# Relative scores of the first cross stream in nine full runs of 512 columns instead of twelve chunks, staged in four slots

## The reference, cut to what matters

```python
q = (einsum('bsd,ed->bse', query, Wq) + bq).reshape(B, S, H, dh).transpose(0, 2, 1, 3)   # H = 16, dh = 32; k and v alike
QEr  = einsum('bhsd,ld->bhsl', q, Er)          # relative scores: row s against all 1024 distances
Srel = _skew(QEr)                              # shifts row s so that distances become key positions
attn = (einsum('bhsd,bhtd->bhst', q, k) + Srel) / sqrt(dh)
attn = softmax(where(causal, attn, -inf))      # causal: key t <= query s
out  = einsum('bhst,bhtd->bhsd', attn, v)
```

## Time and profile before

| | us |
|---|---|
| median of 3 runs | 4168.61 (4167.6 to 4168.93) |
| span of the profiled execution, first to last instruction | 4166.1 |
| PE busy in it | 3837.0 (92%) |
| DVE busy | 2484.1 (60%) |
| ACT busy | 1563.3 (38%) |
| POOL busy | 908.5 (22%) |
| mean granted TensorE clock, as a share of full speed | 0.977 |

### The profile page before, as it was taken

The page is one execution under the profiler, slowest core; times in us unless marked ns, Lnnn a source line. Parts: engine busy times, 40 slices in busy tenths (PEclk is TensorE's granted clock), DMA queues, the critical chain, the costliest instruction groups (busy, mean ns, idle before and its releaser), DMA issues. The chain is left out here.

```text
span 4166.1 us, 90771 instructions
## 1 busy us (share of the span) xinstructions
PE 3837.0 (92%) x36668; PEld 2320.9 (56%) x36668; DVE 2484.1 (60%) x4832; ACT 1563.3 (38%) x3158; POOL 908.5 (22%) x1023
## 2 busy tenths in 40 slices
PE   5999998989999989999999899999998948999995
PEld 2667644656775456567754565677545623444442
DVE  3777535877774358777744587777445872222224
ACT  2444224854442257544422575444135730000002
POOL 2333100223331002233310022333100202222221
PEclk8999999999999999999999999999999978999998
DMA  8333349744333497443335963433359624666667
GB/s 257 109 94 96 119 177 337 234 132 112 96 96 109 189 337 229 131 115 95 95 102 198 344 224 119 115 95 95 102 216 339 221 88 125 157 147 156 149 154 232
DMA packets 325767, 680.63 MB, mean 163 GB/s; under 512 B 28753, under 2 KB 128129, under 8 KB 322129
## 3 DMA queue, kind: packets, MB, share of 16 engines
q1 hardware_dynamic: 272848, 620.60, 46.2%
q0 software_dynamic: 15344, 35.46, 4.6%
q10 hardware_dynamic: 37184, 19.02, 2.1%
HBM read 389.36 MB, written 210.11 MB: 144 GB/s over the span
## 5 line engine op out<-in xcount | busy, mean ns | idle before, releaser
L523 ACT ACTIVATE sc<-sc,nmax 128x1024 f32<-128x1024 f32 x516 | 591.7, 1147 | 774.7 <-DVE nmax L749 774.2
L480 POOL TENSOR_SCALAR sc<-sc,pinv 128x1024 f32<-128x1024 f32 x516 | 576.5, 1118 | 1196.2 <-DVE pinv L757 1183.0
L1081 PE MATMUL psum<-pts,wct 32*64 32x256 f32 x8192 | 460.2, 376 | 9.2 <-PEq L1076 5.2
L1081 PE MATMUL psum<-xall,wct 32*64 32x256 f32 x8192 | 458.7, 376 | 6.9 <-issue 6.8
L1066 PE MATMUL psum<-xt,w_all 128*128 128x256 f32 x1792 | 415.7, 385 | 23.5 <-PEq L1063 23.5
L879 DVE CUSTOM_DVE_ANT_0 sc<-psum,big 128x896 f32<-128x896 f32 (+7 forms) x512 | 364.0, 753 | 104.7 <-PE psum L1287 89.5
L774 DVE STREAM_TRANSPOSE pts<-sc 128x1024 f32<-128x1024 f32 (+3 forms) x342 | 333.6, 976 | 128.2 <-PE psum L1081 84.8
L1066 PEld LDWEIGHTS psum<-xt,w_all 128*128 128x128 f32 x1792 | 332.5, 190 | 128.2 <-issue 66.9
L523 ACT ACTIVATE sc<-sc,xmax 128x896 f32<-128x896 f32 (+7 forms) x512 | 394.8, 773 | 11.7 <-DVE xmax L879 11.6
L749 DVE CUSTOM_DVE_ANT_0 sc<-psum,table_a 128x1024 f32<-128x1024 f32 x258 | 312.1, 1210 | 111.7 <-PE psum L1024 95.9
L1081 PEld LDWEIGHTS psum<-pts,wct 32*64 32x64 f32 x8192 | 310.4, 132 | 100.1 <-issue 55.2
(11 more groups left out here) (175 smaller groups left out, 5242.4 us busy)
## 6 DMA issues: line engine op xcount, KB each, us to landing
wct<-xall SPq DMA_DIRECT2D x576, 128.0 KB, 2.4
big<-skew_d SPq DMA_DIRECT2D x48, 1024.0 KB, 5.9
w_sb<-w_dram SPq DMA_DIRECT2D x48, 1024.0 KB, 5.5
big<-skew_d SPq DMA_DIRECT2D x48, 768.0 KB, 4.4
big<-skew_d SPq DMA_DIRECT2D x32, 896.0 KB, 4.6
big<-skew_d SPq DMA_DIRECT2D x32, 640.0 KB, 5.4
w_all<-wqkv_dram SPq DMA_DIRECT2D x33, 512.0 KB, 3.6
skew_d<-pts SPq DMA_DIRECT2D x8, 2048.0 KB, 6.6
```

What stands on the lines that cost most here:

```text
L480: pool.tensor_scalar(sc[k % 4][:, :], sc[k % 4][:, :], pinv[:, k % 4:k % 4 + 1], 1.0, ALU.mult, ALU.mult).then_inc(probs_scaled, 1)
L523: act.activation(tile, tile, ACT.Exp, bias=least, scale=-1.0, accum_out=total).then_inc(probs_ready, 1)
L1081: mm = pe.matmul(OSUM[HEAD[h], a, :], v_all[rows, ST * (b % GROUPS) + b // GROUPS, HEAD[h]], ptf[h][rows, QG * b:QG * b + QG], start=(b == ...
```

## The change

The 12 chunks of a quad become 9 runs (RUNS), each with exactly 512 columns of PSUM. Six runs are a whole piece of one tile as before. Three runs join pieces of two tiles: 384 columns of tile 6 with the first 128 of tile 4, 256 of tile 5 with the 256 of tile 1, 384 of tile 2 with the 128 of tile 0. The products are the same 12 pieces a quad. Ahead of every run TensorE makes two eighths (FILL = 2): 36 runs, the same 72 eighths. ACT and DVE copy a joined run in two instructions and signal once, behind the second.

The stores are bound to runs (REL_STORES): tile 7 behind run 1, tile 6 behind run 3, tiles 5 and 1 behind run 5, tile 4 behind run 6, tile 3 behind run 7, tiles 2 and 0 behind run 8 (the last). The staging has four slots (REL_SLOT), each used twice a quad: `pts` for tiles 7 and 4, `wct` for 6 and 3, columns 0 to 767 of `big[4:8]` for 5 and 2, and columns 768 to 1023 of it for 1 and 0. The two waits ahead of the second stream change with them: ACT and DVE wait for slots 0 and 1 in full, SP for slots 2 and 3 in full before the load of unit 2. The loads of units 0 and 1 stay behind the last store of the second quad. The diff, without what only renames counts (copy_rel of ACT has the same edit as that of DVE):

```diff
-REL_ORDER = [7, 6, 5, 4, 3, 2, 1, 0]
-CHUNKS = [(t, n) for t in REL_ORDER for n in range(0, P * (t + 1), HALF)]
-NCH = len(CHUNKS)
-FILL = [2 if min(HALF, P * (t + 1) - n) == HALF else 1 for t, n in CHUNKS] * QUADS
-FILLED = [sum(FILL[:kk]) for kk in range(len(FILL) + 1)]
+RUNS = [[(7, 0, 512)], [(7, 512, 512)], [(6, 0, 512)], [(6, 512, 384), (4, 512, 128)], [(5, 0, 512)],
+        [(5, 512, 256), (1, 0, 256)], [(4, 0, 512)], [(3, 0, 512)], [(2, 0, 384), (0, 0, 128)]]
+NRUN = len(RUNS)
+REL_STORES = [(1, (7,)), (3, (6,)), (5, (5, 1)), (6, (4,)), (7, (3,)), (8, (2, 0))]
+REL_SLOT = {7: (0, 0), 4: (0, 1), 6: (1, 0), 3: (1, 1), 5: (2, 0), 2: (2, 1), 1: (3, 0), 0: (3, 1)}
+FILL = 2
+SPLIT = 6 * P
...
-        rel_stored = [sem(f"rel_stored{i}") for i in range(3)]
+        rel_stored = [sem(f"rel_stored{i}") for i in range(4)]
...
-            return next((r for r in range(3, len(BLOCKS)) if FILLED[kk] < ST * (r - 2) <= FILLED[kk + 1]), None)
+            done = FILL * (kk + 1)
+            return 2 + done // ST if done % ST == 0 else None
+
+        def rel_slot(t):
+
+            return relb[min(REL_SLOT[t][0], 2)][:, :, 0 if t > 1 else SPLIT:S]
+
+        def rel_uses(qd, t):
+
+            return 2 * qd + REL_SLOT[t][1]
+
+        def pieces(j):
+
+            return [(t, n, m, sum(p[2] for p in RUNS[j][:i])) for i, (t, n, m) in enumerate(RUNS[j])]
...
-                    made = qd * ST + REL_ORDER.index(t)
-                    sp.wait_ge(rel_stored[made % 3], 16 * (made // 3 + 1))
+                    sp.wait_ge(rel_stored[REL_SLOT[t][0]], 16 * (rel_uses(qd, t) + 1))
...
-                for v in range(XV):
-                    t = REL_ORDER[v % ST]
-                    w = width(t)
-                    made = NCH * (v // ST) + max(j for j in range(NCH) if CHUNKS[j][0] == t) + 1
-                    sp.wait_ge(rel_by_act, made)
-                    sp.wait_ge(rel_by_dve, made)
-                    sp.dma_start(skew_d[v - v % ST + t, 0:HPQ * P * w].rearrange("(h p n) -> p h n", h=HPQ, p=P),
-                                 relb[v % 3][:, :, 0:w]).then_inc(rel_stored[v % 3], 16)
-                    if v == 2 * ST - 1:
+                for qd in range(QUADS):
+                    for j, tiles in REL_STORES:
+                        sp.wait_ge(rel_by_act, NRUN * qd + j + 1)
+                        sp.wait_ge(rel_by_dve, NRUN * qd + j + 1)
+                        for t in tiles:
+                            w = width(t)
+                            sp.dma_start(skew_d[qd * ST + t, 0:HPQ * P * w].rearrange("(h p n) -> p h n", h=HPQ, p=P),
+                                         rel_slot(t)[:, :, 0:w]).then_inc(rel_stored[REL_SLOT[t][0]], 16)
+                    if qd == 1:
                         load_skewed(0)
                         load_skewed(1)
-                sp.wait_ge(rel_stored[2], 16 * len(range(2, XV, 3)))
+                sp.wait_ge(rel_stored[2], 16 * 2 * QUADS)
+                sp.wait_ge(rel_stored[3], 16 * 2 * QUADS)
...
-                        sp.wait_ge(rel_stored[1], 16 * len(range(1, XV, 3)))
+                        sp.wait_ge(rel_stored[1], 16 * 2 * QUADS)
...
-                act.wait_ge(rel_stored[0], 16 * len(range(0, XV, 3)))
+                for i in range(2):
+                    act.wait_ge(rel_stored[i], 16 * 2 * QUADS)
...
-                    t, n = CHUNKS[j]
-                    v, m = qd * ST + REL_ORDER.index(t), min(HALF, width(t) - n)
-                    dve.wait_ge(rel_for_dve, NCH * qd + j + 1)
-                    if v >= 3:
-                        dve.wait_ge(rel_stored[v % 3], 16 * (v // 3))
-                    dve.tensor_copy(relb[v % 3][:, 2:4, n:n + m], psum[:, 6:8, 0:m]).then_inc(rel_by_dve, 1)
+                    dve.wait_ge(rel_for_dve, NRUN * qd + j + 1)
+                    for t, n, m, at in pieces(j):
+                        if rel_uses(qd, t) > 0:
+                            dve.wait_ge(rel_stored[REL_SLOT[t][0]], 16 * rel_uses(qd, t))
+                        ins = dve.tensor_copy(rel_slot(t)[:, 2:4, n:n + m], psum[:, 6:8, at:at + m])
+                    ins.then_inc(rel_by_dve, 1)
 
                 copy_block(1)
...
-                dve.wait_ge(rel_stored[0], 16 * len(range(0, XV, 3)))
+                for i in range(2):
+                    dve.wait_ge(rel_stored[i], 16 * 2 * QUADS)
...
-                    t, n = CHUNKS[j]
-                    w, k = width(t), NCH * qd + j
-                    m = min(HALF, w - n)
+                    k = NRUN * qd + j
                     if j == 0:
                         pe.wait_ge(*evacuated(BLOCKS.index((0, qd))))
                     pe.wait_ge(rel_by_act, k)
                     pe.wait_ge(rel_by_dve, k)
-                    for h in range(HPQ):
-                        mm = pe.matmul(psum[:, 4 + h, 0:m], xq[DH * h:DH * h + DH, qd, P * t:P * t + P],
-                                       er_sb[DH * h:DH * h + DH, S - w + n:S - w + n + m], start=True, stop=True)
-                        if h == 1:
-                            mm.then_inc(rel_for_act, 1)
+                    for t, n, m, at in pieces(j):
+                        first, last = S - width(t) + n, at + m == HALF
+                        for h in range(HPQ):
+                            mm = pe.matmul(psum[:, 4 + h, at:at + m], xq[DH * h:DH * h + DH, qd, P * t:P * t + P],
+                                           er_sb[DH * h:DH * h + DH, first:first + m], start=True, stop=True)
+                            if last and h == 1:
+                                mm.then_inc(rel_for_act, 1)
                     mm.then_inc(rel_for_dve, 1)
...
                 for qd in range(QUADS):
-                    for j in range(NCH):
-                        kk = NCH * qd + j
-                        for i in range(FILLED[kk], FILLED[kk + 1]):
+                    for j in range(NRUN):
+                        for i in range(FILL * (NRUN * qd + j), FILL * (NRUN * qd + j + 1)):
                             project_eighth(3 + i // ST, i % ST)
                         relative(qd, j)
```

More of the change, by code:

```diff
@@ L455, in _ @@
                 sp.sem_inc(x2_ready, -1)
-                for i in range(3):
-                    sp.sem_inc(rel_stored[i], -16 * len(range(i, XV, 3)))
+                for i in range(4):
+                    sp.sem_inc(rel_stored[i], -16 * 2 * QUADS)
                 def store_rows(dst):
@@ L634, in copy_rel @@
                 def copy_rel(qd, j):
[L636 to L641 removed]
+                    act.wait_ge(rel_for_act, NRUN * qd + j + 1)
+                    for t, n, m, at in pieces(j):
+                        if rel_uses(qd, t) > 0:
+                            act.wait_ge(rel_stored[REL_SLOT[t][0]], 16 * rel_uses(qd, t))
+                        ins = act.copy(rel_slot(t)[:, 0:2, n:n + m], psum[:, 4:6, at:at + m])
+                    ins.then_inc(rel_by_act, 1)
                 root_of_variance()
@@ L1361, in _ @@
                 pe.sem_inc(ot_scaled, -XV)
[L1362 to L1363 removed]
+                pe.sem_inc(rel_by_act, -NRUN * QUADS)
+                pe.sem_inc(rel_by_dve, -NRUN * QUADS)
                 for c in range(DC):
```

23 lines of the change are left out of this document (8 added, 15 removed).

## The result

The changed kernel takes 4183.64 us (median of 5 runs, 4181.85 to 4186.94); the kernel before, on the same chip, 4168.93 (5 runs, 4167.6 to 4172.29). The ratio is 1.0036, with a 95% interval of 1.0023 to 1.0048. The forecast was 4153, its range 4133 to 4176.

The account below looks back on a forecast made before the run. PE, busy 92% of the span, was taken as the bound, with DMA 81% busy in the stage. 12.6 won - 6.0 store waits - 2.4 border = 4.2 us a batch, 16 in all: 4153 us, range 4133 to 4176.

Parts of the forecast that it names:

- PE's side: Relative-product stage: fewer alternations, joined groups costing 0.1 us each; 107.6 us without other holds, 12.6 us a batch won.
- Tile 7's store before run 4: In the stage, tile 4's first copy waits for this store to free the slot; 0.7 us lost in every quad.
- waits of copies other than tile 4's: Sign in the changed kernel's profile that would show the forecast wrong; no size given.
- The queue: Stores between quads: queue runs to 31.7 us, next tile 7 starts at 33.1; waits including tile 7's, 6.0 us a batch.
- an odd late store: In the stage's store queue: delays about once a quad, 0 to 1.8 us each, taken as 1.2, sometimes two.
- The clock: Rival: the third quad's wait lowers PE's clock, costing 5 us a batch there and about 2 at the border; chance 0.10.
- The border: Start of the second stream: first addition loses 0.8 us and unit 2 1.6; together 2.4 us a batch, bounds 0 and 5.
- the first addition: Start of the second stream: waits for tiles 4 and 3, 5.6 us behind the last product, a loss of 0.8.
- unit 2's load: Second stream: waits for tiles 2 and 0, issued at 8.5 us, takes 3.4; unit 2's addition 12.7, loss 1.6.
- later units have more room: Second stream behind unit 2: the forecast put no loss on these units.
- The DMA holds only 357 GB/s: Rival: stage unchanged at 120 us, border 4 worse, -3.8 us a batch, 4184 us; chance 0.05.
- PE's clock falls: Rival: third quad's wait brings the low clock, 5 us a batch plus about 2 at the border, 4188 us; chance 0.10.

Follow-up runs that it names:

- run 3: Not a follow-up run: in each quad of the changed kernel, the joined piece of 384 columns of tile 6 and the first 128 of tile 4; not timed alone.
- run 5: Not a follow-up run: in each quad of the changed kernel, the joined piece of 256 columns of tile 5 and 256 of tile 1; not timed alone.
- no slot wait: Changed kernel with tile 4's last 128 columns copied to tile 1's place, so no copy waits for tile 7's store (output partly wrong): 4141.2 us.
- the new order: Changed kernel with its nine runs and slots reordered, one semaphore a tile, and the loads of units 0 and 1 split between two quads: 4145.4 us, ratio 0.9948.
- late waits: Changed kernel with ACT and DVE waiting for the stores from `pts` and `wct` only where units 1 and 3 first need them: 4185.1 us.
- Unit 2 freed: Changed kernel with late waits, plus units 2 and 3 loaded into `xt`, so that they wait for no store out of `big`: 4173.79 us.
- loads later: Changed kernel with the loads of units 0 and 1 issued behind tile 7's store of the third quad: 4160.98 us, ratio 0.9986.
- the new order with late waits: The new order, with ACT and DVE waiting for `pts` only ahead of unit 1 and `wct` only ahead of unit 3: 4139.25 us, ratio 0.9935.

## Why the prediction was wrong, point by point

- **PE's side: right.** Forecast 107.6 us without waits, measured 106.7 (no slot wait). The joined group costs 0.01 us instead of 0.1. The 12.6 us a batch to be won are there: the new order has them nearly all (stage 107 to 108 against 119.9).
- **Tile 7's store before run 4: right in place, and in size with an empty queue.** 0.7 was foretold for the first quad and 0.65 measured. It is the largest wait that the change adds to the stage, but not the only one. Tile 7's own copy waits for tile 4's store, 0.9 to 1.1 us a batch, which the sum put at nothing and which the prediction named among the signs of being wrong ("waits of copies other than tile 4's").
- **The queue: the step that failed in the stage.** "12.6 + 0.5 + 18.6 = 31.7" with "1.4 us of slack" puts tile 5 right behind tile 6, at 17.6 us into the quad. But the store of tiles 5 and 1 goes out only behind run 5; the prediction itself has 18.7 for it in its part on the second stream. The second quad shows the gap, 1.2 us without a byte. That alone takes nearly all of the slack. Tiles 5 to 0 and the two loads then took about 18.0 us (611.2 to 629.2) where the sizes at 0.41 MB/us and the 2.4 of the loads make 16.5, as narrower rows move slower; the widest, tiles 7 and 6, were sized right. And tile 7's last bytes took 2 us at 35 GB/s. Against all this stood 1.2 us for an odd late store. So the third quad's wait was 5.08 instead of 3.0, and the waits of a batch 8.4 on average (8.7 in the first) instead of 6.0.
- **The clock: put at nothing in the sum, and half right as a rival.** The third quad's wait did bring the low clock, for 3.4 us in three batches and 6.8 in one. In the first batch it cost 1.7 us and not 5, because the low stretch was shorter than the one behind the border.
- **The border: the term that failed most.** Forecast 2.4 us a batch, measured 5.8 from the last product's end. Of its two parts the first addition didn't decide. It was put at 5.6 behind the last product and came there in two batches and at 7.2 in two, whose borders were no longer (23.4 and 23.2 against 24.2 and 23.7), and late waits brought it to 3.8 and won nothing. The part that failed is unit 2's load. It was put at 8.5 and came at 9.8, took 4.3 instead of 3.4 to land, and its addition stood at 15.0 instead of 12.7. About 1 us more was lost behind unit 2, where "later units have more room" put nothing; its cause isn't shown. The low clock at the border grew from 10.2 us to 13.7 in the first batch. Unit 2 freed shows that 2.6 us are the wait for the last stores. That the bytes still in the queue hold the other part of the delay of unit 2 is argued from how late its load lands, and no run took bytes away to test it.
- **The sum.** Forecast 12.6 - 6.0 - 2.4 = 4.2 a batch to win. The stage gave 3.1 in the first batch (120.2 less 117.1), which is 12.6 and 0.9 more, less 8.7 of waits and 1.7 of clock, and 3.0 on average. The border took 5.8 and the rest 0.7, of which no cause is shown; it differs in sign between the batches. Together that is 3.5 us a batch lost.
- **The loads of units 0 and 1: seen, and too small.** Their 2.4 us were in the forecast of the third quad's wait. By loads later they cost 5.5 a batch, as they fall on a queue with no slack, and their wait brings the low clock with it.
- **Two rivals met the time by luck.** "The DMA holds only 357 GB/s", at 0.05, gave 4184, and "PE's clock falls", at 0.10, 4188; measured was 4183.64. The first left the stage unchanged and lost 4 us at the border, where the stage won 3.0 and the border lost 5.8; and with no slot wait DMA let the stage run in 106.7 us. The second had 5 us of low clock in the stage, where the first batch shows 1.7.

## What to carry to other kernels

Before a buffer is given to the next tile sooner, follow the queue ahead of the store that frees it. Add up its bytes, at the rate that a window with rows of their width shows, and give each store the time at which it can be issued at the earliest: a gap in the queue is lost for good, here 1.2 us of a slack of 1.4. Where no slack is left, a load issued in between falls on the critical path. A faster stage hands its backlog to whatever comes next: look at which first load of the next stage waits behind the last store. A wait taken away there may for the most part move into the queue: here a load issued 6.4 us sooner gave its mask 2.2 us sooner. And a load moved ahead of a store delays all that waits for this store. The gain was real and could be had with the same nine runs: at least two runs between a store and the reuse of its place instead of one, a semaphore for each tile, and the two loads apart from each other and away from the store with the least room.

## What the runs showed of the hardware

- The rate of a DMA queue that isn't empty went with the width of the rows. Over the first stage of the changed kernel a packet of 4096 bytes took 162 ns on average, one of 3584 bytes 140, of 2048 bytes 85, of 1536 bytes 68, of 1024 bytes 51 and of 512 bytes 30; on 16 engines that makes 405, 409, 383, 361, 323 and 271 GB/s. The windows above agree: 417 GB/s with rows of 4096 bytes, 286 with rows of 512 and 1024.
- 1.05 MB added to a full queue moved the landing behind them by 3.0 to 3.2 us with rows of 2048 bytes, and by 3.0 to 4.2 with rows of 512.
- A store behind a full queue can end in a tail. Of the third quad's tile 7 in the first batch the last bytes took 2 us at 35 GB/s. What holds them isn't shown.
- Issuing on SP gets slower as the queue fills: a pair of stores took 0.91 us at 671.00, in the new order with late waits, and 1.88 at 619.32 in the changed kernel, with the stores of tiles 4 and 3 ahead of it still under way; a pair of loads 2.85, and 3.83 behind the added wide store, where before the change it took 1.16.
- A wait of 5.08 us on PE was followed by a run of 4.64 us instead of 2.98 at the lower of the two clock levels (1.2 and 2.4 GHz) for part of it; waits of up to 1.7 us left the granted clock of the whole stage at 1.00.
